# Four graph layers in one kernel: rows, residual and layer norm in one phase by pieces, and all weights loaded at the start

## What is computed

```python
x = _layernorm(x + _L0_gnn_ref(x, ...))   # three attention layers, each with a batch norm over the nodes
x = _layernorm(x + _L1_gnn_ref(x, ...))   # batch norm, gather, w1, batch norm, w2, gather, batch norm
x = _layernorm(x + _L2_gnn_ref(x, ...))   # attention with four heads for each of three relations
x = _layernorm(x + _L3_gnn_ref(x, ...))   # q, k, v; attention over keys; wo, batch norm, w1, w2, batch norm
```

## Time and profile before

| | |
|---|---|
| median of three runs | 2724.74 us |
| the profiled execution | 2725.16 us |
| its span in the trace | 2723.3 us |
| DVE busy | 2161.7 us (79%) |
| PE busy | 2103.4 us (77%) |
| ACT busy | 1860.7 us (68%) |
| mean granted TensorE clock | 0.89 |

### The profile page before, as it was taken

How to read it: one execution, slowest core, us unless ns; L and a number is a source line. 1 busy time by engine, 2 the same in 40 slices (tenths; PEclk the granted TensorE clock), 3 DMA queues, 4 the chain that set the end, 5 groups by cost and what they waited for, 6 DMA issues and landing times. The chain is left out here.

```text
span 2723.3 us, 90169 instructions
## 1 busy us (share of the span) xinstructions
PE 2103.4 (77%) x33923; PEld 1853.3 (68%) x33923; DVE 2161.7 (79%) x4355; ACT 1860.7 (68%) x3006; POOL 86.7 (3%) x137
## 2 busy tenths in 40 slices
PE   3999997698698698395938999489976989567544
PEld 3655554598598597394927999389875889566522
DVE  6999996788788788515078999899988999759943
ACT  5999997675775775202059999699969999445431
POOL 1111111000000000000000000000000000000000
PEclk8999998899899899697978999799988999788767
DMA  3354554342342341272722331333304332043100
GB/s 85 158 225 196 206 224 196 120 142 65 114 150 62 119 148 59 86 220 66 236 80 83 113 100 35 101 106 95 95 21 129 96 95 83 4 140 121 41 9 24
DMA packets 182241, 302.56 MB, mean 111 GB/s; under 512 B 6394, under 2 KB 158845, under 8 KB 181976
## 3 DMA queue, kind: packets, MB, share of 16 engines
q1 hardware_dynamic: 181191, 297.57, 33.0%
q0 software_dynamic: 800, 1.26, 0.2%
HBM read 214.26 MB, written 84.54 MB: 110 GB/s over the span
## 5 line engine op out<-in xcount | busy, mean ns | idle before, releaser
L430 ACT ACTIVATE stage<-ps 125x375 f32 x625 | 313.9, 603 | 38.1 <-PE ps L376 33.8
L331 DVE TENSOR_SCALAR col<-iota_col,window_col 125x376 bf16<-125x376 f16 x1250 | 310.0, 318 | 3.6 <-PE ps L376 3.6
L376 PE MATMUL ps<-col,lo 125*125 125x375 bf16 x1250 | 290.3, 345 | 17.5 <-DVE col L331 17.2
L931 ACT ACTIVATE r1amsk<-r1ad,r1thr 125x640 f16 x360 | 259.6, 816 | 0.1
L931 ACT ACTIVATE r2amsk<-r2ad,r2thr 125x640 f16 x360 | 259.6, 814 | 0.1
L931 ACT ACTIVATE r0amsk<-r0ad,r0thr 125x640 f16 x360 | 259.6, 814 | 0.1
L1004 PE MATMUL ps<-r1mv,r1asel 125*128 125x66 f16 x5000 | 244.4, 196 | 4.8 <-issue 3.5
L1004 PE MATMUL ps<-r2mv,r2asel 125*128 125x66 f16 x5000 | 242.7, 196 | 2.4 <-issue 1.3
L1004 PE MATMUL ps<-r0mv,r0asel 125*128 125x66 f16 x5000 | 242.8, 196 | 1.1 <-DVE r0asel L953 0.5
L376 PEld LDWEIGHTS ps<-col,lo 125*125 125x125 bf16 x1250 | 136.9, 139 | 144.5 <-DVE col L331 141.4
L1004 PEld LDWEIGHTS ps<-r1mv,r1asel 125*128 125x128 f16 x5000 | 227.4, 100 | 8.7 <-issue 4.0
(11 more groups left out here) (537 smaller groups left out, 4412.5 us busy)
## 6 DMA issues: line engine op xcount, KB each, us to landing
counts<-stage SPq DMA_DIRECT2D x75, 800.0 KB, 4.8
ct<-counts_all SPq DMA_DIRECT2D x75, 800.0 KB, 4.6
counts_all<-total SPq DMA_DIRECT2D x25, 800.0 KB, 7.3
g0ct<-counts_all SPq DMA_DIRECT2D x25, 800.0 KB, 4.7
g1ct<-counts_all SPq DMA_DIRECT2D x25, 800.0 KB, 4.6
g2ct<-counts_all SPq DMA_DIRECT2D x25, 800.0 KB, 4.6
r0ct<-counts SPq DMA_DIRECT2D x25, 800.0 KB, 4.7
r1ct<-counts SPq DMA_DIRECT2D x25, 800.0 KB, 5.3
```

The costliest lines, as they stand in the source:

```text
L331: ins = v.tensor_scalar(col1[:, b % OHS * WIN + w], K.iota_col[:], K.window_col[:, bass.ds(i * (P // DG) + b, 1), w], None, ALU.is_equal)
L376: ins = pe.matmul(K.ps[0:P, s, 0:GW], lo1[:, b, 0:P, w], col1[:, s * WIN + w, 0:GW], start=(w == 0), stop=(w == WIN - 1))
L430: act.activation(dst.rearrange("p a r h d -> p (a r h) d"), K.ps[0:P, b % OHS, 0:GW].rearrange("p (x d) -> p x d", d=DG), ACT.Copy).then_i ...
L931: act.activation(msk[:, s % 5, n], ad[:, bass.ds(g % 2, 1), h] .rearrange("p a (b d) -> p (a b) d", d=PAD), ACT.Sigmoid, bias=T.thr[:, 1, ...
```

## The change

`turn_to_rows` with residual, `layer_norm` and the turn back or the store become one phase, `rows_norm`. The residual is no longer added by VectorE: TensorE multiplies the block of `K.zT` by the identity (a plain product that gives the rows) and accumulates the identity times `x[:, k]` on top. The statistics read PSUM; so does the scaling, which writes `K.x`. The blocks go in three pieces, 0 to 11, 12 to 19, 20 to 24; ScalarE scales blocks 0 to 15 and 24, VectorE 16 to 23. With `dst` TensorE turns each piece back when it is scaled and the two engines move the banks to `K.zT`; with `store` SP stores each piece in two transfers, of partitions 0 to 111 and 112 to 124. ln2 has no `cols` and reads `K.x` in SBUF. `batch_norm` b1 now finds `K.zT` filled.

All weights stay in SBUF from the preparation on: eight transfers on SP behind the wait for the keys' store. `above` and `win` share one room in SBUF to make space. `load`, t4 and t5 are gone.

```diff
 def prepare(nc, K, S):
+        shared_room = sb("above", [P, 10313], F32)
+        above = shared_room[:].bitcast(F16)[:, 0:NCH // SUB * NG].rearrange("p (c g) -> p c g", c=NCH // SUB)
+        win = shared_room[:, 0:DG * WIN * CH * 2].rearrange("p (j w e k) -> p j w e k", j=DG, w=WIN, e=CH)
...
                 sp.wait_ge(keys_out, 32)
+                for dst, src in ((K.w1[:], K.w1_in.rearrange("f (j o) -> f j o", j=2)),
+                                 (K.w2[:], K.w2_in.rearrange("(j f) o -> f j o", j=2)),
+                                 (K.wqkv[:, 0:D], K.wq_in), (K.wqkv[:, D:2 * D], K.wk_in), (K.wqkv[:, 2 * D:3 * D], K.wv_in),
+                                 (K.wo[:], K.wo_in), (K.fw1[:], K.fw1_in.rearrange("f (j o) -> f j o", j=4)),
+                                 (K.fw2[:], K.fw2_in.rearrange("(j f) o -> f j o", j=4))):
+                    sp.dma_start(dst, src).then_inc(weights, 16)
                 sp.wait_ge(consts, 80)
+                sp.wait_ge(weights, 128)
...
-def layer_norm(nc, K, S, tag, x):
+def rows_norm(nc, K, S, tag, x, cols=None, dst=None, store=None):
+    PIECES = ((0, 12), (12, 20), (20, NB))
+    by_act = lambda k: k < 16 or k == 24
...
+        read = lambda k: x[:, k] if cols is None else K.ps[0:P, k // 4, k % 4 * D:(k % 4 + 1) * D]
+        done_a = lambda k: sum(by_act(i) for i in range(k))
+        moved_by_act = lambda m: m % 2 == 1
+            @block.tensor
+            def _(pe):
+                if cols is not None:
+                    for k in range(NB):
+                        out = K.ps[0:P, k // 4, k % 4 * D:(k % 4 + 1) * D]
+                        pe.matmul(out, cols[:, k * P:(k + 1) * P], K.ident[:], start=True, stop=False)
+                        pe.matmul(out, K.ident[0:P, 0:P], x[:, k], start=False, stop=True).then_inc(summed, 1)
+                if dst is not None:
+                    for k0, k1 in PIECES:
+                        pe.wait_ge(by_a, done_a(k1))
+                        pe.wait_ge(by_v, k1 - done_a(k1))
+                        for k in range(k0, k1):
+                            pe.transpose(K.ps[:, k // 4, k % 4 * P:(k % 4 + 1) * P], x[:, k], K.ident[0:P, 0:P]
+                                         ).then_inc(turned, 1)
...
             @block.vector
+                def statistics(p):
+                    k0, k1 = PIECES[p]
+                    for k in range(k0, k1):
+                        if cols is not None:
+                            v.wait_ge(summed, min(k // 4 * 4 + 4, NB))
+                        ins = v.bn_stats(st[:, k], read(k))
+                    link(ins)
+                    for k in range(k0, k1):
+                        ins = v.bn_aggr(mv[:, k], st[:, k])
+                    link(ins)
+                    v.tensor_scalar(mv[:, k0:k1, 1], mv[:, k0:k1, 1], EPS, None, ALU.add).then_inc(known, 1)
+
+                def scale(p):
+                    k0, k1 = PIECES[p]
+                    v.wait_ge(rstd, p + 1)
+                    link(v.reciprocal(mv[:, k0:k1, 1], mv[:, k0:k1, 1]))
+                    v.scalar_tensor_tensor(shift[:, k0:k1], mv[:, k0:k1, 0], -1.0, mv[:, k0:k1, 1], ALU.mult,
+                                           ALU.mult).then_inc(scaled, 1)
+                    for k in range(k0, k1):
+                        if not by_act(k):
+                            v.tensor_scalar(x[:, k], read(k), mv[:, k, 0:1], mv[:, k, 1:2], ALU.subtract,
+                                            ALU.mult).then_inc(by_v, 1)
+
+                statistics(0)
+                for p in range(3):
+                    if p < 2:
+                        statistics(p + 1)
+                    scale(p)
+                if dst is not None:
+                    for m in range(7):
+                        if not moved_by_act(m):
+                            v.wait_ge(turned, min(4 * m + 4, NB))
+                            v.tensor_copy(*column_move(m))
...
             @block.scalar
+                for p, (k0, k1) in enumerate(PIECES):
+                    act.wait_ge(known, p + 1)
+                    act.activation(mv[:, k0:k1, 1], mv[:, k0:k1, 1], ACT.Sqrt).then_inc(rstd, 1)
+                    act.wait_ge(scaled, p + 1)
+                    for k in range(k0, k1):
+                        if by_act(k):
+                            act.activation(x[:, k], read(k), ACT.Identity, bias=shift[:, k:k + 1],
+                                           scale=mv[:, k, 1:2]).then_inc(by_a, 1)
...
+            if store is not None:
+                @block.sync
+                def _(sp):
+                    rows = store.rearrange("(b p) f -> p b f", p=P)
+                    for k0, k1 in PIECES:
+                        sp.wait_ge(by_a, done_a(k1))
+                        sp.wait_ge(by_v, k1 - done_a(k1))
+                        for h in (slice(0, 112), slice(112, P)):
+                            sp.dma_start(rows[h, k0:k1], x[h, k0:k1]).then_inc(stored, 16)
+                    sp.wait_ge(stored, 32 * len(PIECES))
...
 def build(nc, args, out):
-            turn_to_rows(nc, K, "r0", K.zT, K.x, residual=K.x)
-            layer_norm(nc, K, "ln0", K.x)
+            rows_norm(nc, K, "ln0", K.x, cols=K.zT, dst=K.zT)
...
-            batch_norm(nc, K, "b1", K.zT, K.zT, col("g_in"), col("be_in"), rows=K.x)
+            batch_norm(nc, K, "b1", K.zT, K.zT, col("g_in"), col("be_in"))
...
-            turn_to_rows(nc, K, "r2", K.zT, K.x, residual=K.x)
-            layer_norm(nc, K, "ln1", K.x)
-        turn_to_columns(nc, K, "t4", K.x, K.zT)
+            rows_norm(nc, K, "ln1", K.x, cols=K.zT, dst=K.zT)
...
-        layer_norm(nc, K, "ln2", K.x)
-        turn_to_columns(nc, K, "t5", K.x, K.zT)
+        rows_norm(nc, K, "ln2", K.x, dst=K.zT)
...
-                turn_to_rows(nc, K, "r3", K.zT, K.x, residual=K.x)
-                layer_norm(nc, K, "ln3", K.x)
-                sp.dma_start(out.rearrange("(b p) f -> p b f", p=P), K.x[:]).then_inc(stored, 16)
-                sp.wait_ge(stored, 16)
+                rows_norm(nc, K, "ln3", K.x, cols=K.zT, store=out)
```

More of the change, by code:

```diff
@@ L229, in _ @@
                 v.wait_ge(gathered, 16 * DG)
[L230 removed]
+                cols = win.rearrange("p j w e k -> p j (w e) k")[:, :, :, 1]
                 ins = v.tensor_tensor(cols, cols, gb[:].unsqueeze(2).to_broadcast([P, DG, WIN * CH]), ALU.subtract)
@@ L1381, in _ @@
                     v.tensor_tensor(dst[:, b, 0:W], K.ps[0:P, b % 8, 0:W], bias, ALU.add).then_inc(taken, 1)
-@phase
-def load(nc, K, S, tag, pairs):
-    landed = S(tag + "_landed")
-    with nc.Block() as block:
-        @block.sync
-        def _(sp):
-            for dst, src in pairs:
-                sp.dma_start(dst, src).then_inc(landed, 16)
-            sp.wait_ge(landed, 16 * len(pairs))
 STEEP = 1.0e8
```

61 lines of the change are left out of this document (21 added, 40 removed).

## The result

The changed kernel took 2716.54 us as the median of 18 runs (2707.3 to 2723.3), beside 2730.22 for the kernel before in the same comparison (2721.8 to 2753.9), 13.7 less. The means, 2715.4 and 2732.3, are 17.0 apart; their ratio is 0.9938 with an interval of 0.9917 to 0.9959. So the change takes off 14 to 17 us; forecast were 20.0. The profiled run took 2711.62 us, its span is 2709.8, against 2723.3 before: 13.5 less.

A forecast was written before the change was run, and what follows sets the result against it. The kernel was taken as a row of phases with barriers, no one engine bounding all. Gains 0.4 - 0.7 + 3.7 + 2.7 + 4.4 + 9.5 = 20.0 us took the median from 2724.74 to 2704.7, range 2697 to 2713.

The forecast's parts named there:

- The untouched stages: Stages the diff leaves alone, over 90% of the span: taken as unchanged; a changed length would show the prediction wrong.
- I take it as kept: r0s after ln1: TensorE's clock survives a gap widened from 0.8 to about 2.1 us; otherwise 1.9 us are lost.
- The rival tied this to l3: The clock is not kept: l3 and r0s both start at 1.2 GHz, 2.7 + 1.9 us more, 2709.3; chance 15%.
- l3's clock: At l3's start: transposes end only 1.3 us before it, so it keeps the higher clock; gain 2.7 us.
- ln0 and ln1: Fused phases with residual: ln0 29.8 against 30.2 us, gain 0.4; ln1 26.0 against 25.3, loss 0.7.
- its margin: Around the 2704.7 us forecast: +/- 3 us for the clock's rise; a phase ends 0.9 earlier or 0.4 later.
- The rival's 0.26 per block of ScalarE: ScalarE scaling out of PSUM is cheap, 0.26 instead of 0.386 us per block: 7.5 us less, 2697; chance 10%.
- That in ln0 the removed load pays for a slower turn: ln0 to b1: removed load of w1 and w2, transposes and b1's refill pay for the slower turn; gain 0.4 us.
- The loads ahead of t6: Before t6: without the load of wo and fw, the first transpose comes 0.3 us after the last reduction; gain 4.4.
- the store: ln3 and the kernel's end: pieces stored at 269 GB/s instead of 109, 26.2 us against 35.7; gain 9.5.
- ln2: Row phase without product ahead of l3: 17.9 us against 21.6, load of wqkv included; gain 3.7.
- The weights in the preparation cost nothing: Eight loads in the preparation end by 33 us, before the gathers start at 37.33; cost 0, up to 7 if on the path.

The follow-up runs named there:

- the second comparison: The unchanged changed kernel timed again against the kernel before: 2708.96 us beside 2724.57, ratio 0.9944.
- the four padded runs: Idle one-element products added in the preparation: 64 to the kernel before, 32, 64 or 128 to the changed kernel; the three relations took 925.9 to 930.2 us in sum.
- again_before: The kernel before, unchanged, profiled a second time; its three relations took 921.6 us in sum, its l3 18.05 us.
- early: Changed kernel with the residual added by VectorE, pieces scaled behind their own statistics, later roots between ScalarE's blocks, blocks divided anew; ratio 0.9861 to the kernel before.

## Why the prediction came out as it did

The sign and the order of size held; the time of 2716.5 lies 3.5 above the upper end of 2713, the second comparison's 2709.0 inside the range. That the first lies outside is in part the level of its comparison (5.5 us), which no step of the prediction bears on.

- **The untouched stages, put at nothing in the sum, are the step that failed.** The prediction named a changed length there as what would make it wrong, but gave it no price and no rival. The relation loops lost 7.9 us in the first pair of profiles, 3.0 in the second and 7.0 on the mean of seven, because the new list of TensorE moved the stands at issue by about 20 products and made them longer (the count of products and the four padded runs). The counting moved by 2.5 us either way, by chance.
- **"I take it as kept" (r0s' clock) failed**: the gap was 2.2 us, as forecast (2.1), and that was too long. The price was 1.5, not 1.9. The rival tied this to l3; the two came apart, since l3's gap shrank to 0.97.
- **l3's clock came out in size (2.8 for 2.7), in part by luck**: against *again_before* the same gain is 1.7. The prediction put the shorter gap down to the new order as a whole; it comes with the load's removal, and the row phase alone left the gap at 4.34.
- **ln0 and ln1, terms mis-sized**: +1.5 and +1.2 for +0.4 and -0.7. In ln1 ScalarE began 12.8 us after the first product (forecast 13.7; it was 14.0 in ln0 and 14.1 in ln3), because the clock rose about 3 us into the burst instead of about 6 (its windows of 1 us have 0.50 in 1377 to 1378, 0.82 in the next and then 1.00; in ln3 the step lies at 2689, 5.8 after the start); the prediction had put this rise into its margin. A block of ScalarE out of PSUM took 0.35 (twelve in 4.29 less four in 1.50, by 8), not 0.386. So the turn back ran from 17.2 to 21.8 (forecast 18.4 to 23.8) and the moves ended at 22.9, not 24.9. VectorE's blocks out of PSUM took 0.32 ((1.36 less 0.40)/3) where 0.256 had been taken, but there are only four in a piece. The rival's 0.26 per block of ScalarE was too low. The two errors in ln0 and ln1 make the sum of the touched stretches larger than forecast, so they hid part of the loss.
- **That in ln0 the removed load pays for a slower turn was right**: the phase alone is 1.4 slower there, and the removed load of w1 and w2 carries 3.0. That ln1 would be no shorter than before was wrong, by the 1.2 above.
- **The loads ahead of t6 and the store were right, ln2 nearly so**: 4.4 for 4.4, 9.1 for 9.5, 4.5 for 3.7; one transfer of 125 partitions costs the 12.3 us against six that its expectation put at 12.5.
- **The weights in the preparation cost nothing**, as said: issued from 26.5 to 30.2, and the counting began at 58.4 in both.

On the two prices of a scaled block out of PSUM the Trainium skill (Perfetto Trace Analysis, Optimizing Scalar/DVE Operations) gives an overhead per operation of about 93 ns for ScalarE on SBUF and 51 on PSUM, and of 60 and 125 ns for VectorE; taken from the rows of SBUF, an estimate of 0.34 and 0.32 us. The trace agrees with 0.35 and 0.32, and both would have been a better middle than the values that the prediction took.

## What to carry to other kernels

Before forecasting a gain of a few tenths of a per cent, look at the loops that are not touched: where a loop body is many packets of instructions long and TensorE bounds it, adding instructions anywhere ahead can cost or give some us (here the sum of three loops lay between 917 and 932), and a few padded copies of the kernel before, profiled, show how much. Read a phase's order for the first instruction of the second engine: scaling each piece behind its own statistics, with the blocks divided anew, was worth 10.8 us in four phases, the cheaper residual 6.1. A load that stands between two bursts of TensorE costs its own time and can cost the clock of what follows (here with a gap of 4.3 us).

## What the runs showed of the hardware

- TensorE's loop of 2500 instructions is fetched again in each round, 11 packets of 16.4 KB in the round that was counted. Some 443 to 450 products into a round, with the loads of scores and counts under way, TensorE stands for 0.7 to 2.0 us; the stand is gone with either load. Shortly behind the jump back it stands for 2.1 to 2.7 us even with both loads cut or those of the counts alone, and up to 3.4 with them. Both depend on where the loop lies: 12, 16 and 32 more products ahead of it moved them by 12, by 15 or 16, and by 31 products, and 256 instructions more brought the pattern back.
- The granted clock outlasted ln1's burst until just before a gap of 2.2 us ended; gaps of 0.81, 1.13 and 1.65 kept it, gaps of 2.14 to 2.23 lost it, for 1.5 to 1.7 us over the next 50 products.
- The counting, untouched in all kernels, took 421.1 to 424.1 us, and 432.5 once (in the profile of *early*).
